# Presort of a graph kernel: high and low part of the running cell ends in one operand of 113 rows

## The reference, cut to what matters

```
h = jnp.maximum(_layernorm(x, axis=-1), 0.0)
msg = jax.nn.relu(h[src] + edge_attr @ We + be)           # layer 0
aggr = jax.ops.segment_sum(msg, dst, num_segments=N)
...                                                        # layer 1: two GCN convolutions
agg = jax.ops.segment_sum(transformed[etype, src] * norm, dst, num_segments=N)   # layer 2, twice
out = spmm(out) * 0.9 + h * 0.1                            # layer 3, ten times
```

## Time and profile before

| what | us |
|---|---|
| median of 3 runs | 8985.64 |
| the profiled execution | 9017.37 |
| its span (first to last instruction) | 9015.5 |
| until the first scatter | 157.10 |
| from the first to the 17th run of scatters | 1406.20 |
| everything after 1800 us | 7215.50 |

### The profile page before, as it was taken

One profiled execution on the slowest core, in us unless ns is written; L12 is line 12 of the kernel. 1 busy time (PEld: TensorE's weight loads), 2 busy tenths in 40 slices (PEclk: granted clock), 3 DMA queues, 4 the chain that ended last, 5 costly groups with the idle time before them and its releaser, 6 DMA issues.

```text
span 9015.5 us, 140479 instructions
## 1 busy us (share of the span) xinstructions
PE 5276.5 (59%) x47086; PEld 4379.6 (49%) x47087; DVE 2679.7 (30%) x5950; ACT 1586.1 (18%) x3420; POOL 3320.8 (37%) x3295
## 2 busy tenths in 40 slices
PE   4535444256655557874333335333332999999998
PEld 3323222133333336863332234323322999999998
DVE  4100000277777663232222223222223211111111
ACT  1112111003455541011111111111110000000000
POOL 2354454555555430005566653665664000000000
PEclk7555555577777777986565567566665999999999
DMA  6111111622333333433222224222222666666665
GB/s 238 38 42 42 37 45 46 57 62 73 80 82 83 83 55 130 148 111 93 64 58 59 66 57 116 59 66 57 59 59 35 200 199 199 198 198 199 199 198 166
DMA packets 531454, 914.61 MB, mean 101 GB/s; under 512 B 223435, under 2 KB 365788, under 8 KB 530220
## 3 DMA queue, kind: packets, MB, share of 16 engines
q1 hardware_dynamic: 285688, 621.27, 22.4%
q0 software_dynamic: 104896, 162.89, 8.8%
q10 hardware_dynamic: 140646, 128.06, 4.6%
HBM read 705.38 MB, written 205.67 MB: 101 GB/s over the span
## 4 chain that ended last, share of the span: by engine, by line
PE 50%; issue 18%; another core or an unknown queue 17%; DVE 7%; DVEq 3%; ACT 3%; DMA 1%; POOL 0%; ACTq 0%; SPq 0%; POOLq 0%
PE bank L1343 26%; PE bank L1226 7%; PE bank L1297 4%; DVEq L513 2%; PE bank L1070 2%; PE bank L1368 1%; PE bank L1322 1%; PE bank L1215 1%; PE bank L1361 1%; DVE edge_sums L1766 1%; PE bank L1132 1%; ACT staged_records L830 1%; PE bank L1120 1%; PE bank L1135 1%
## 5 line engine op out<-in xcount | busy, mean ns | idle before, releaser
L731 POOL DMA_INDIRECT rows<-relation_table,staged_rows x1664 | 1681.5, 1011 | 1941.3 <-DMA staged_rows<-table_rows_of_tiles 1451.6
L1343 PE MATMUL bank<-own_term,h_transposed 128*128 128x192 f16 x16464 | 1377.7, 247 | 105.4 <-DMA h_transposed<-edge_counts 60.6
L1343 PEld LDWEIGHTS bank<-own_term,h_transposed 128*128 128x128 fp8e4 x16464 | 1364.3, 98 | 106.8 <-issue 106.0
L731 POOL DMA_INDIRECT rows<-node_table,records_in x832 | 882.2, 1060 | 766.0 <-PE bank L1215 515.4
L716 POOL DMA_INDIRECT rec_dst<-staged_records,staged_record_rows x781 | 750.9, 961 | 906.0 <-ACT staged_record_rows L839 522.5
L1343 PE MATMUL bank<-own_term,staged_records 128*128 128x192 f16 x12348 | 1032.4, 246 | 0.0
L1343 PEld LDWEIGHTS bank<-own_term,staged_records 128*128 128x128 fp8e4 x12348 | 1020.0, 98 | 0.0
L1766 DVE TENSOR_TENSOR edge_sums<-edge_sums,bank 128x96 f32 x1664 | 421.4, 253 | 1990.8 <-PE bank L1297 1604.4
L1368 PE MATMUL bank<-ones,staged_records 128*128 128x1 bf16 x2401 | 137.9, 165 | 1203.8 <-issue 990.2
L1297 PE MATMUL bank<-rows,onehot 128*128 128x96 f32 x3328 | 592.0, 348 | 301.9 <-issue 150.0
L992 ACT CAST staged_records<-bank 128x512 fp8e4<-128x512 f32 (+1 forms) x637 | 336.8, 565 | 2284.6 <-PE bank L1361 1234.2
(11 more groups left out here) (310 smaller groups left out, 6150.8 us busy)
## 6 DMA issues: line engine op xcount, KB each, us to landing
h_transposed<-edge_counts SPq DMA_DIRECT2D x280, 784.0 KB, 4.2
staged_records<-edge_counts SPq DMA_DIRECT2D x210, 784.0 KB, 4.2
h_transposed<-edge_counts_T SPq DMA_DIRECT2D x56, 784.0 KB, 4.3
rec_dst<-records_in SPq DMA_DIRECT2D x80, 520.0 KB, 10.8
records_in<-rec_dst SPq DMA_DIRECT2D x104, 400.0 KB
edge_counts_T<-staged_records ACTq DMA_DIRECT2D x343, 112.0 KB
staged_records<-edge_counts_T ACTq DMA_DIRECT2D x49, 784.0 KB
edge_counts<-staged_records ACTq DMA_DIRECT2D x49, 784.0 KB
```

The source lines that it names most:

```text
L731: pool.indirect_dma_start(out=rows[:, g, j, 0:D], out_offset=None, in_=source, in_offset=at(ap=index(g, j), axis=0)).then_inc(gathered[g], 16)
L1343: last = nc.tensor.matmul(banks[j][:, 0:2 * D], slots[c][:, at:at + P], z[:, c * SB + i, :], start=(c == 0 and i == 0), stop=(c == SG - 1 ...
```

## The change

Both parts of the cell ends are put into one operand: the high part in partitions 0 to 48, the low part in partitions 64 to 112, and zeros in 32 to 63 before the high part is written, so that the unused partitions 49 to 63 hold no garbage. The one-hot table gets the same two halves: `load_blocks` broadcasts to 113 partitions, and `block_columns` compares partition p with p, or with p - 64 from 64 on (`block_no`). One product over 113 rows then takes the place of the two over 49. `compare` still reads 49 rows.

```
-        ends_hi = halves(acc, 0, SG * ECP)[0:NB, :].rearrange("p (g c) -> p g c", g=SG)
-        ends_lo = halves(flat, 0, SG * ECP)[0:NB, :].rearrange("p (g c) -> p g c", g=SG)
+        LOW = P // 2
+        BOTH = LOW + NB
+        cell_ends_of = halves(acc, 0, SG * ECP).rearrange("p (g c) -> p g c", g=SG)
+        ends_hi = cell_ends_of[0:NB, :, :]
+        ends_lo = cell_ends_of[LOW:BOTH, :, :]
...
             def load_blocks(c0, n):
-                act.dma_start(block_T[0:NB, 0:n * P], block_dram[c0:c0 + n, :].rearrange("(a c) p -> a (c p)", a=1)
-                              .broadcast_to([NB, n * P])).then_inc(block_row_in, 16)
+                act.dma_start(block_T[0:BOTH, 0:n * P], block_dram[c0:c0 + n, :].rearrange("(a c) p -> a (c p)", a=1)
+                              .broadcast_to([BOTH, n * P])).then_inc(block_row_in, 16)
...
-                        a = block_T[0:NB, c * P:(c + 1) * P]
-                        nc.tensor.matmul(to, a, ends_hi[:, :, number * QC + c], start=False, stop=False)
-                        last = nc.tensor.matmul(to, a, ends_lo[:, :, number * QC + c], start=False,
-                                                stop=True)
+                        a = block_T[0:BOTH, c * P:(c + 1) * P]
+                        last = nc.tensor.matmul(to, a, cell_ends_of[0:BOTH, :, number * QC + c], start=False, stop=True)
...
+            then(V.tensor_scalar(block_no[:, :], part_no[:, :], float(LOW), -float(LOW), ALU.is_ge, ALU.mult))
+            then(V.tensor_tensor(block_no[:, :], block_no[:, :], part_no[:, :], ALU.add))
+            then(V.memset(acc[LOW // 2:LOW, 0:SG * ECP // 2], 0.0))
...
-                V.tensor_scalar(block_T[0:NB, 0:columns * P], block_T[0:NB, 0:columns * P], part_no[0:NB, 0:1], None,
+                V.tensor_scalar(block_T[0:BOTH, 0:columns * P], block_T[0:BOTH, 0:columns * P], block_no[0:BOTH, 0:1], None,
                                 ALU.is_equal).then_inc(block_T_ready, 1)
```

More of the change, by code:

```diff
@@ L279, in build @@
         part_no = sb("partition_number", [P, 1])
+        block_no = sb("block_of_partition", [P, 1])
         cell_tot = sb("cell_total", [NB, SG])
```

## The result

The changed kernel takes 9040.69 us in the median of 6 runs (9028.08 to 9055.58), the kernel before 8995.10 beside it (6 runs, 8981.37 to 9012.94): a ratio of 1.0049, 95% interval 1.0034 to 1.0064, 46 us slower. The forecast was 9105. Its profiled execution took 9055.58, with a span of 9053.8.

What follows compares the result with a forecast made beforehand. No engine was full, so the order of waits, chiefly PE's counts held while scatters run, was taken to set the time. Start +110, load 3 +38 and beats -28 gave +120 us, put on the median as 9105 us (range 9035 to 9170).

Steps and rivals of the forecast that it cites:

- the load: Block-number load to 113 partitions: all rows on one DMA engine, 51.4 us quiet to 70.4 us crowded.
- the start: Up to the first scatter: late loads 1 and 2 make records ready last, first scatter at 267.8 instead of 157.1, +110 us.
- load 3: First beat: load issued at P + 63.8 as before, 45.6 us longer, groups 7.6 less, +38 us.
- the 14 steady beats: Late load nearly hidden by the hold, no group passing before it; 2 us saved a beat, -28 us.
- the last stretch: The last, shorter stretch after the steady beats: no change, 0 us.
- load 2: Second block-number load, at the start: crowded by the zeros, 70.4 us, landing at 252.6 instead of 133.9.
- the hold: PE's counts come late while scatters run: two within 25 us of a beat's first scatter (P), others by about P + 61.9.
- the column: Narrow products per column in `find_places`: 0.10 us instead of 0.27, two at 0.05 each, giving a group 1.48 instead of 2.17.
- rival 3: Steps of rows stay in `find_places`: a column costs 0.22 us, 5.3 us more a beat, 9195 us; chance 8%.
- Rival 2: The hold lets more through: load 3 at -8, beats at -4.9, +33 in all, 9019 us; chance 10%.
- Rival 4: The load comes after the hold: at 0.65 us a row a beat is 8.4 us longer, 9223 us; chance 7%.
- Rival 1: The load is spread over 7 or 16 engines, at most 10 us: -89 us, 8897 us; chance 11%.

Runs made afterwards that it cites:

- first_loads: Changed kernel with its first three block-number loads sent to 128 partitions, the other 15 still to 113; 8958.97 us, ratio 0.9858 to the kernel before.
- alternate_again: Kernel before, three products kept, every second column taking its 128-row product last; on a chip with a hold, 9033.16 us, ratio 0.9941.
- spread_128: Changed kernel with every block-number load sent to 128 partitions instead of 113; on the chip without a hold, 7895.45 us, ratio 0.9998 to the kernel before.
- spread_again: The same kernel as spread_128, rerun on a chip with a hold; 8948.15 us, ratio 0.9826 to the kernel before.
- load_only: Kernel before with only the load widened to 113 partitions, 64 never read, three products kept; chip without a hold, 8404.21 us, ratio 1.0651.
- compare_113: spread_128 with compare also reading 113 rows and ACT's bias -2; on a chip with a hold, 8898.51 us, ratio 0.9772 to the kernel before.
- alternate: Kernel before, three products kept, every second column taking its 128-row product last; on the chip without a hold, 7885.05 us, ratio 0.9994.

## Why the prediction was wrong, step by step

| step | forecast | measured |
|---|---|---|
| the load: one engine, 0.43 us a row | 51.4 to 70.4 us | 67.2, 59.0, 49.6; 57 in the beats |
| the start, to the first scatter | +110 | +98.7 |
| load 3 | +38 | +36.3 |
| the 14 steady beats | -28 | -85.7 |
| the last stretch | 0 | -3.5 |
| behind the 17th run | 0 | -7.5 |
| sum, profiled executions | +120 | +38 |

**The load was right.** One engine, by the pattern of three counts; 113 packets with one report against 128 with 16. The Trainium skill's rule ("DMA: Bandwidth & Descriptors", Why a DMA increments its semaphore by 16 and not by 1) gives the same counts for both.

**The start was right but for its second load.** I let the zeros crowd load 2 to 70.4 us; it took 59.0, which is the size of the 11 us between +110 and +98.7. SP's queue moved only 0.40 MB beside it, so the zeros were over. Load 1 was 3.2 us shorter than forecast, and the way from load 2 to the first scatter 2.7 longer. first_loads shows that the start is where the change loses: without the three slow loads the 2nd run of scatters begins 161 us earlier, part of it because load 3 then goes out before the hold.

**Load 3 was right** in its time, issued at P + 65.2 and 49.6 us to DVE, though eight clippings of that beat had passed before the hold ended: the last three set the time.

**The steady beats failed**, and with them the forecast: they gave 57.7 of the 82 us between +120 and +38. The step that failed is the sentence that none of the groups gets through before the hold, and with it the term of 9 groups at 1.48 us behind the hold, where 7 at 1.29 stood. Two groups got through in every beat; the forecast had named a clipping of group 0 before P + 55 as the sign of this, and it came at P + 52.0. I put the next load at P + 77.4; it went out at P + 72.9. Of these 4.5 us, two groups that passed at P + 52.0 and 55.4 are 2 x 1.48 = 3.0, and 7 groups at 1.29 instead of 1.48 another 1.3; 0.2 are left. That the load's lateness is nearly hidden in the beats stood (80.89 and, in first_loads, 80.82 with late loads, 79.71 with all loads early). What passes the hold was at hand: the forecast itself says that two counts get through in the first 25 us of a beat, and I took that for a matter of the time since P. In the steady beats it is two or three counts wherever the work starts (three in 6 of the 14 beats before, two in all 14 after); the first beat of the changed kernel, with eight, shows that this is no rule. For the column I took the pitch in place, 0.05, over the 0.027 of the earlier trace rows, which was right: 0.053 a column. 49-row neighbours stand 0.05 apart just behind a step, and 0.03 otherwise, as alternate_again shows. The bounds of the beats, -2.1 and +5.3 us, were reckoned with all 11 groups and not with the 9 behind the hold; with 9 they are -1.7 and +4.3, and rival 3 comes to some 9181 us and not 9195. The last two rows of the table, 11 us together, were put at nothing. The 3.5 of the last stretch are probably its shorter groups again; the 7.5 behind the 17th run were not looked into.

**Rival 3**, that steps of rows stay, is out: a column with one product less is 0.053, with a third one kept 0.08. The rule of the Trainium skill that changing the tiling mode drains the array ("TensorEngine Tiling", Key Properties) agrees with all four kernels: 0.12 and 0.10 where 49 rows meet 128, nothing to see between 113 and 128. The column of 0.21 us that the prediction set against the earlier trace rows is not seen. **Rival 2** was half true: more got through in the beats; in the first one eight groups did, but not the last three, since the load itself came too late for them to end by P + 16. With the load spread it was true there too (-27 us). **Rival 4** needed the load behind P + 62; it landed at P + 49. **Rival 1**, that the load is spread, was no rival here, but it priced spread_128 on the low side: it said -89 us and spread_again measured -156, since the first beat gained 27 and not 3, and the beats 6.9 and not 5.9. These are 38 of the 67 us; the rest is open, as the kernel before was not traced on that chip.

**What was not foreseen** is that the answer depends on the chip. Where counts are held, the change is 0.3 to 0.5% slower (1.0049, 1.0034, 1.0039). Where they are not, load_only is 6.5% slower, and the changed kernel, which was not run there, should lose some 4 to 5% (an estimate, not shown: load_only's 518 us less 17 stretches of 11 groups, 0.88 us each, is 353 us, 4.5%).

**Left open** is why counts come late while GpSimd scatters on some chips. Shown: PE's are late for ACT and for DVE alike, DVE's own are slowed too, in the steady beats they come with the end of the scatters, and one chip doesn't do it. In the one beat in which the scatters paused the clippings passed at once (compare_113). What lets two, three or eight counts through an unbroken run I can't say.

## What to carry to other kernels

Before a product is widened to merge two, count what its operand's load becomes: 113 partitions went over one DMA engine, and the first three such loads cost 161 us; 128 partitions, 15 of them unread, took that back and made the same edit 1.7% faster than before on a chip with a hold, and neither faster nor slower on the one without. In rows of narrow products it is the change of the row count between neighbours that costs, not one product more, so order or pad them to equal rows, the wide products beside them too. And where a wait of unknown cause covers a cost, say what the cost is without it: here the cover was absent on one of the four chips of the experiments.

## What the runs showed of the hardware that I had not expected

- The same program takes 7886 us on one chip and 8995 to 9104 on the others. Of these 1100 to 1200 us, some 480 are the presort's (its last scatter ends at about 1182 us in alternate, a kernel of the same time on that chip, and at 1663 in the kernel before on the chip of the result); the others lie behind it, and were not looked into.
- Where counts are held, 49 short DVE instructions that each send a count and wait for none stand mostly 0.7 or 1.4 us apart instead of 0.16, while scatters run. When two scatters took 5.46 and 7.22 us instead of 0.96, 11 counts of PE's passed with no delay.
- A step between 49 and 128 rows costs 0.10 to 0.12 us between narrow products against 0.027 between equals, and 0.12 to 0.14 around the 512-wide product. 113 and 128 rows count as equal.
- A load of 113 rows of 11 KB takes 57 us, one of 128 rows about 6.
